# Replacing half of a router kernel's TensorE transposes by a second load and VectorE block turns

## The reference

```python
W = weights[condition]                               # 64 batches choose among 16 matrices, 128x128
h = einsum('bct,bcd->bdt', x, W)                     # per batch 128x2048
flat = h.reshape(8192, 2048)
logits = einsum('th,eh->te', flat, router_weight) + router_bias       # 64 experts
scores = softmax(logits)
topk_w, topk_idx = top_k(scores, 8)
w_sum = topk_w.sum(-1)
bias_mix = w_dense @ expert_bias                     # w_dense: scores kept at the 8 places, else 0
out = x + flat * w_sum + bias_mix
```

## Time and profile before

| | |
|---|---|
| time, three runs | 589.59 to 590.24 us, median 589.76 |
| profiled execution | 590.77 us, of which the span from first to last instruction is 589.0 |
| busy in the span | PE 569.0 us (97%), DVE 419.8 (71%), ACT 367.6 (62%), POOL 378.9 (64%) |
| DMA | 137.09 MB; packets fill 63.6% of the 16 engines' span |
| mean granted TensorE clock | 0.989 of full speed |

### The profile page before, as it was taken

The page is one execution under the profiler, slowest core; times in us unless marked ns, Lnnn a source line. Parts: engine busy times, 40 slices in busy tenths (PEclk is TensorE's granted clock), DMA queues, the critical chain, the costliest instruction groups (busy, mean ns, idle before and its releaser), DMA issues.

```text
span 589.0 us, 12871 instructions
## 1 busy us (share of the span) xinstructions
PE 569.0 (97%) x3600; PEld 503.8 (86%) x3600; DVE 419.8 (71%) x996; ACT 367.6 (62%) x773; POOL 378.9 (64%) x391
## 2 busy tenths in 40 slices
PE   5769999999999999999999999999999999999996
PEld 5768888888898888888988888888888888888874
DVE  2757776777777767777767777677777776777764
ACT  3656665676665676666667666566666566666651
POOL 0257666767666766666766766676766676666675
PEclk9879999999999999999999999999999999999998
DMA  8915666676676676676666566667567657666244
GB/s 272 343 68 213 250 243 224 249 257 221 238 271 215 226 285 212 233 267 226 232 255 242 221 249 252 221 239 268 217 227 280 217 226 274 224 233 256 107 174 184
DMA packets 28867, 137.09 MB, mean 233 GB/s; under 512 B 3314, under 2 KB 3314, under 8 KB 20722
## 3 DMA queue, kind: packets, MB, share of 16 engines
q1 hardware_dynamic: 28850, 136.88, 63.6%
HBM read 69.76 MB, written 67.11 MB: 232 GB/s over the span
## 4 chain that ended last, share of the span: by engine, by line
PE 95%; ACT 1%; DVE 1%; DMA 1%; issue 1%; ACTq 0%; DVEq 0%
PE zt_ps L279 21%; PE xt_ps L266 19%; PE p_ps L327 10%; PE p_ps L332 10%; PE p_ps L329 10%; PE p_ps L333 10%; PE p_ps L328 10%; PE scores_ps L302 2%; PE scores_ps L311 1%; PE scores_ps L293 1%; DMA x_sb<-L_ffn_router_weight 1%; ACT xt_hi L378 0%; DVE xt_lo L467 0%; PE p_ps L341 0%; DVE e_kept L501 0%
## 5 line engine op out<-in xcount | busy, mean ns | idle before, releaser
L601 POOL TENSOR_TENSOR x_lo<-x_sb,x_hi 128x512 fp32r<-128x512 f32 x256 | 325.0, 1292 | 163.7 <-ACT x_hi L386 161.5
L467 DVE TENSOR_TENSOR xt_lo<-xt_ps,xt_hi 128x512 fp32r<-128x512 f32 x256 | 176.1, 688 | 140.1 <-ACT xt_hi L378 139.9
L378 ACT CAST xt_hi<-xt_ps 128x512 fp32r<-128x512 f32 x256 | 149.9, 587 | 164.5 <-PE xt_ps L266 158.5
L522 DVE SCALAR_TENSOR_TENSOR out_sb<-p_ps,w_sum,x_sb 128x512 f32<-128x512 f32 x256 | 190.0, 742 | 11.6 <-PE p_ps L333 9.9
L266 PE MATMUL xt_ps<-ident,x_sb 128*128 128x128 f32 x1024 | 155.2, 276 | 0.3 <-DMA x_sb<-x 0.3
L266 PEld LDWEIGHTS xt_ps<-ident,x_sb 128*128 128x128 f32 x1024 | 124.0, 142 | 13.0 <-DMA x_sb<-x 0.5
L386 ACT CAST x_hi<-x_sb 128x1024 fp32r<-128x1024 f32 x128 | 134.0, 1048 | 0.7 <-PE p_ps L333 0.7
L279 PE MATMUL zt_ps<-xt_hi,router_hl 128*128 128x256 f32 x512 | 129.5, 285 | 1.3 <-DVE xt_lo L467 1.3
L279 PE MATMUL zt_ps<-xt_lo,router_hl 128*128 128x256 f32 x512 | 129.2, 284 | 0.0
L327 PE MATMUL p_ps<-x_hi,w_hl 128*128 128x512 f32 x256 | 121.6, 475 | 0.1
L279 PEld LDWEIGHTS zt_ps<-xt_hi,router_hl 128*128 128x128 f32 x512 | 97.8, 191 | 7.1 <-DVE xt_lo L467 1.5
(11 more groups left out here) (40 smaller groups left out, 330.8 us busy)
## 6 DMA issues: line engine op xcount, KB each, us to landing
out<-out_sb SPq DMA_DIRECT2D x128, 512.0 KB, 3.5
x_sb<-x SPq DMA_DIRECT2D x62, 1024.0 KB, 5.6
x_sb<-x SPq DMA_DIRECT2D x4, 512.0 KB, 7.0
out_sb<-L_ffn_expert_bias SPq DMA_DIRECT2D x2, 512.0 KB, 11.6
x_sb<-L_ffn_router_weight SPq DMA_DIRECT2D x1, 512.0 KB, 5.6
bias_sb<-L_ffn_router_bias SPq DMA_DIRECT2D x1, 32.0 KB, 8.8
cond_sb<-itok_B SPq DMA_DIRECT2D x1, 0.2 KB
out_sb<-L_cond_weights SPq DMA_DIRECT2D x1, 0.5 KB, 10.7
```

The lines of the kernel that those rows point to most:

```text
L378: act.copy(xt_hi[:, n % 2, :, r, :], xt_ps[v % 4][:, :].rearrange("p (q c) -> p q c", c=P)).then_inc(xt_hi_ready, 1)
L467: dve.tensor_tensor(xt_lo[:, n % 2, :, r, :], xt_ps[v % 4][:, :].rearrange("p (q c) -> p q c", c=P), xt_hi[:, n % 2, :, r, :].bitcast(F32) ...
L522: dve.scalar_tensor_tensor(out_sb[:, r, cols], p_ps[n % 2][:, :], w_sum[:, o % 2, r:r + 1], x_sb[:, (2 * o + r) % XRING, cols], ALU.mult, ...
L601: pool.tensor_tensor(x_lo[:, r, cols], x_sb[:, (2 * o + r) % XRING, cols], x_hi[:, r, cols].bitcast(F32), ALU.subtract).then_inc(x_lo_read ...
```

## The change

`RELAID` = 2 of the four pieces of each batch, columns 1024 to 2047, are no longer turned by TensorE. SP loads these columns a second time into `x_turn`, in four transfers per pair (`load_turned`): transfer `a` writes the 32 partitions from 32a on, and partition 32a + c holds channels c, 32 + c, 64 + c and 96 + c of both batches, columns 1024 + 256a to 1024 + 256a + 255, in runs of 1 KB. VectorE's `relay` then turns 32x32 blocks of it into the same PSUM banks (128 partitions by 512 elements per instruction). Its innermost step through `x_turn` is 8 elements, since neighbouring partitions of the result hold columns that lie 8 apart. The router's matrix is prepared in the matching order.

```diff
+RELAID = 2
...
+    PLAIN = PIECES - RELAID
+    RUN = RELAID * P
+    GROUPS = C // 32
...
+        x_turn = sb("x_turn", [P, 2, 2, GROUPS, RUN])
...
+            x_pairs = x.rearrange("(i r) (g c) t -> i c (r g) t", r=2, c=32)
+
+            def load_turned(m, o):
+                i = 4 * m + o
+                wait(sp, relaid_in_ps, 2 * RELAID * (i - 1))
+                for a in range(GROUPS):
+                    t0 = PLAIN * PIECE + a * RUN
+                    sp.dma_start(x_turn[32 * a:32 * (a + 1), o % 2, :, :, :].rearrange("p r g s -> p (r g) s"),
+                                 x_pairs[i, :, :, t0:t0 + RUN]).then_inc(x_turn_loaded[o % 2], 16)
...
                     for r in range(2):
                         load(m, i, r)
+                        if r == 0:
+                            load_turned(m, i)
                         store(m, i - 3, r)
...
                 r, n = v % 2, v // 2
+                if n >= PLAIN:
+                    return
...
+                if t < PLAIN * BLOCKS:
+                    block_of_router = router_sb[:, t * P:(t + 1) * P]
+                else:
+                    j = t - PLAIN * BLOCKS
+                    block_of_router = router_sb[:, PLAIN * PIECE:T].rearrange("e (k j) -> e j k", k=P)[:, j, :]
+                last = pe.transpose(p_ps[t // (TB // 2)][:, q * E:(q + 1) * E], block_of_router, ident[0:E, 0:E])
...
-                act.wait_ge(xt_in_ps, SLOTS * i + v + 1)
+                if n < PLAIN:
+                    act.wait_ge(xt_in_ps, 2 * PLAIN * i + v + 1)
+                else:
+                    act.wait_ge(relaid_in_ps, 2 * RELAID * i + v - 2 * PLAIN + 1)
...
+            def relay(m, o, v):
+
+                r, k = v % 2, v // 2 - PLAIN
+                i = 4 * m + o
+                if v == 2 * PLAIN:
+                    dve.wait_ge(x_turn_loaded[o % 2], 16 * GROUPS * (2 * m + o // 2 + 1))
+                wait(dve, xt_lo_ready, SLOTS * i + v - 3)
+                dve.transpose(xt_ps[v % 4][:, :].rearrange("p (q g c) -> p q g c", g=GROUPS, c=32),
+                              x_turn[:, o % 2, r, :, :].rearrange("p g (c q) -> p q g c", c=32)[
+                                  :, k * BLOCKS:(k + 1) * BLOCKS, :, :]
+                              ).then_inc(relaid_in_ps, 1)
...
                     if mid and v == 3:
                         top(m, i - 1)
+                    if new and 2 * PLAIN <= v + 2 < SLOTS:
+                        relay(m, i, v + 2)
```

More of the change, by code:

```diff
@@ L121, in adaln_router @@
         first_half_loaded = [sem(f"first_half_loaded{i}") for i in range(2)]
+        x_turn_loaded = [sem(f"x_turn_loaded{i}") for i in range(2)]
         out_stored = [sem(f"out_stored{i}") for i in range(2)]
@@ L140, in adaln_router @@
         xt_in_ps = sem("xt_in_ps")
+        relaid_in_ps = sem("relaid_in_ps")
         xt_hi_ready = sem("xt_hi_ready")
@@ L216, in store @@
                                  out_sb[:, r, h * HALF:(h + 1) * HALF]).then_inc(out_stored[r], 16)
+            x_pairs = x.rearrange("(i r) (g c) t -> i c (r g) t", r=2, c=32)
[6 more added lines that the diff above has]
+                                 x_pairs[i, :, :, t0:t0 + RUN]).then_inc(x_turn_loaded[o % 2], 16)
             sp.dma_start(router_sb, router_weight).then_inc(router_loaded, 16)
             for h, landed in ((0, first_half_loaded), (1, x_loaded)):
+                if h == 1:
+                    load_turned(0, 0)
                 for r in range(2):
@@ L227, in _ @@
             load(0, 1, 1)
+            load_turned(0, 1)
             sp.dma_start(bias_sb[:, :], router_bias.to_broadcast([P, E])).then_inc(bias_loaded, 16)
@@ L232, in _ @@
             load(0, 2, 1)
+            load_turned(0, 2)
             sp.wait_ge(router_in_ps, 1)
@@ L238, in _ @@
                 load(0, 3, r)
+                if r == 0:
+                    load_turned(0, 3)
                 store(0, 0, r)
@@ L340, in _ @@
                 q = t % (TB // 2)
-                last = pe.transpose(p_ps[t // (TB // 2)][:, q * E:(q + 1) * E],
-                                    router_sb[:, t * P:(t + 1) * P], ident[0:E, 0:E])
+                if t < PLAIN * BLOCKS:
[4 more added lines that the diff above has]
+                last = pe.transpose(p_ps[t // (TB // 2)][:, q * E:(q + 1) * E], block_of_router, ident[0:E, 0:E])
             last.then_inc(router_in_ps, 1)
```

## The result

The change takes 660.04 us (median of four runs, 658.28 to 660.48) against 589.67 for the kernel before: a ratio of 1.119, interval 1.117 to 1.121. It is slower by 70 us, where 655 was forecast. The profiled execution took 658.28 us, its span is 656.4, 67.4 more than before.

A forecast was written before the change was run, and what follows sets the result against it. PE bounds the kernel, and the DVE, ACT and POOL chain limits next. Span 589.0 + 42.6 (chain) + 13 (clock) + 9.2 (start-up) = 653.8, plus 0.8 above the span: 655 us, range 603 to 688.

The forecast's parts named there:

- the chain with a quick turn: `keep` held up: Mid-run, `keep` falls behind POOL's `x_lo` start and is held up; period 18.88 us, 1.42 longer, +42.6 us over 30 periods.
- TensorE's clock in mid-run: PE's new waits may bring 1.2 GHz stretches costing 1.3 us each; bounds 0 and 39, a third taken: +13 us.
- start-up and end: In the start-up, two groups of the second load delay the experts' loads on a full queue: 2 x 4.6 = +9.2 us.
- time above the span: Executed time beyond the profiled span, taken from the profile of the kernel before: 0.8 us added.
- B: Cut event in each period: the end of `neg_max`, at 310.36 us in the profile before.
- not held up: Rival: `keep` is not delayed by POOL in mid-run; period 17.03, time 586 us; chance 0.10.
- I take R = 0.65, next to the row of the same engine: One block turn on DVE costs 0.65 us, between bounds 0.61 from `xt_low` and 1.2 from POOL's pace.
- R hardly enters: The turn's price barely affects the period, as `keep` meets POOL's two pieces for any price from 0.34 to 1.5 us.
- From B to A: From `neg_max`'s end to the next step's first `project` matmul waiting for `kept_low`: 8.20 us before, 9.62 forecast.
- each turn costs 1.2: Rival: slow turns also delay slot 7's `xt_low`; period 19.4, time 657 us, up to 39 more by the clock; chance 0.20.
- From A to B: From the first `project` matmul waiting for `kept_low` to `neg_max`'s end, slots 0 to 3: unchanged at 9.26 us.
- Hidden in mid-run: The second load's 4.6 us per pair makes 16.1 us of DMA, hidden unless the period falls below 16.1.

The follow-up runs named there:

- contiguous turn: The change with turns reading x_turn in steps of 1 element instead of 8, the router's matrix reordered to match: 641.16 us, ratio 1.086.
- the run with both edits: The change with turns reading in steps of 1 element and `e_rest` in PSUM instead of SBUF: 587.61 us, ratio 0.996 to the kernel before.
- the fastest version: The change with turns in steps of 1 element, `keep` moved to the end of slot 4, and start-up loads in order of need: 576.79 us, ratio 0.978.
- the run with the early `keep`: The change with `keep` moved from slot 5 to the end of slot 4, turns still at step 8: 629.37 us, ratio 1.069.

## Why the prediction came out as it did

By its own terms, in the spans (589.0 to 656.4):

| term | forecast | measured | from |
|---|---|---|---|
| the chain with a quick turn: `keep` held up | +42.6 (period 18.88) | +38.6 (18.75) | contiguous turn |
| the turn's price above 0.65 | 0 | +18.4 (0.61 x 30) | the change less contiguous turn |
| TensorE's clock in mid-run | +13 | 0 | clock 1.00 from 60 to 630 |
| start-up and end | +9.2 | +10.4, of it 7.4 by the loads alone | spans less 30 periods |
| time above the span | 0.8 | 3.6 | 660.04 - 656.4 |

**Right: the mechanism.** That the bound moves from PE to the chain from `neg_max` to `kept_low`, because `keep` falls behind POOL's start, was read out of one stretch of the start-up, and the runs show it four ways: both `e_kept` are short with an operand in PSUM, short in an earlier place, long where they meet POOL, and then end with a piece of POOL's. The price of the hold-up was nearly right too: with the turn that was assumed (0.65; the contiguous one takes 0.62 from start to start) both `e_kept` are long and the period is 18.75, 0.13 below the forecast. The 3.09 us from POOL's start to `kept_twice` are 2.92 in that run: in the start-up, where the 3.09 were read, POOL's own first piece was held up as well (see the last section). In the change `kept_twice` came at B + 6.06 where 5.94 stood, by two errors that nearly cancel: POOL started 0.27 later, and `kept_twice` followed 2.94 behind it. There only the second `e_kept` is long, and not both, as the prediction's signs had it. And the rival "not held up" is the run with both edits: period 17.03 as worked out, time 587.6 where 586 stood.

**Wrong: the price of a turn.** The step that failed is "I take R = 0.65, next to the row of the same engine". The turn takes 1.09 in the period shown. `keep` met POOL all the same, as the text said for any R from 0.34 to 1.5, but "R hardly enters" does not hold. From B to A the contiguous run needs 9.35 us, the change 9.86. Of these 0.51, 0.30 lie ahead of the reciprocal's end (B + 5.67 and B + 5.97): ACT's `xt_hi` waits 0.17 us for the turn, so POOL itself starts at B + 3.12 instead of 2.84. The other 0.21 come behind it, where a turn stands ahead of slot 7's `xt_low`. So the case that came is the rival "each turn costs 1.2", which had a chance of 0.20, with its period of 19.4 (measured 19.36) and its sign, turns over 1 us; but it put the whole delay behind `keep`, where 0.21 of the 0.51 came. I weighed the step in memory by `z_sum`, which reads PSUM in steps of 64 elements at no loss, and let that row stand for SBUF; the runs with steps of 1, 2, 4 and 8 show that the turn's read of SBUF does not behave like it: 0.71 to 1.17 us.

**Wrong: the clock.** Mid-run, PE waits 0.92 us for `finish` and 1.16 for `kept_twice` in the period shown, and the clock stays at full speed from 60 to 630 us. A third of the pairs was a guess between 0 and all, and 0 is what came. The two wrong terms, 18.4 too little and 13 too much, nearly cancel; that the time came within 5 us is in good part luck. (642 and 39 for the clock are 681; the 682 of the prediction is a slip.)

**The start-up** was right in size (9.2 and 10.4) and half right in cause: the queue is full and the added megabytes delay what stands behind them, but the experts' wait is one of two that end together.

**From A to B** I kept 9.26 us; it is 9.41. The 0.15 us, 4.5 in 30 periods and part of the +38.6, were not followed up. PE's busy time fell by 0.6 us per pair in the change (17.46 to 16.83) and by 1.2 in the fastest version (16.25), where the prediction took off 1.7; no run removes the transposes alone, so what they are worth stays open. **Hidden in mid-run:** the second load was, at 17.46 us as well. It took 5.2 us of all DMA engines per pair, not 4.6, so that they are full at 16.86 and not only below 16.1.

## What to carry to other kernels

Work taken from the bounding engine pays only if the chain that it uncovers has room: before moving work, cut the period at two events and see which short instructions get past a neighbour by a few tenths, as `keep` did by 0.39 us here. A short VectorE instruction with two SBUF operands that meets a long GpSimd row, as `e_kept` did, is held for it; move it ahead, or put one operand in PSUM. Let a block turn read SBUF in steps of at most 8 bytes, and in a start-up load first what is used first: with `keep` ahead of POOL and these two the same idea turned from 12% slower to 2.2% faster.

## What the runs showed of the hardware

A block turn of 128x512 f32 from SBUF to PSUM takes 0.71 to 0.72 us at steps of 4 and 8 bytes, 1.11 at 16, 1.17 at 32, while a reduction that reads PSUM in steps of 256 bytes takes 0.41 us, no more than one of the same size without a step. I had not expected the jump between 8 and 16 bytes to be nearly the whole price.

`e_kept`, 0.22 us by itself, is held until the running POOL instruction ends, and gets in between two of them: 0.85 and 1.30 us in one pair of the contiguous run. The Trainium skill (SBUF — State Buffer, SBUF: two separate sides) calls this a lock that whoever starts first holds for the whole instruction, and counts a VectorE operation with two SBUF inputs among its users; the rows agree, and so does the run with one operand in PSUM, 0.20 and 0.22 us inside POOL's piece.

It goes the other way too, where DVE is first. These rows are from the change's start-up; `out_sb` holds the experts there:

```profile
39.06 2.29 DVE L590 TENSOR_TENSOR expert_hl<-out_sb,expert_hl 64x2048 fp32r<-64x2048 f32 x1
...
39.92 3.78 POOL L649 TENSOR_TENSOR x_lo<-x_sb,x_hi 128x512 fp32r<-128x512 f32 x2 [9.43 <-ACT x_hi L420]
```

The DVE instruction, with two SBUF operands, ends at 41.35. POOL's two pieces take 3.78 us instead of 2.55, the first of them 2.56 us. In the kernel before the same pair of instructions overlaps less, and POOL's row is 2.75.

TensorE's clock: with waits of 0.94 and 0.69 us the run with the early `keep` fell to 1.2 GHz in 3 of 28 pairs, while the change with 0.92 and 1.16 kept 2.4 GHz from 60 to 630 us. The pair after the one shown has waits of 0.95 and 0.71 us and kept 2.4 GHz, so the rows do not tell what does it.
